# A recommender's product tower on one core: constants, first loads and one copy take other places in the queues

## The reference

```python
for W in (W0, W1):
    last = x.shape[1]
    inter = (x[:, :, None, :] * x_emb[:, None, :, :]).reshape(B, last * F, D)
    x = jnp.einsum('bid,hi->bhd', inter, W)
    outs.append(x.sum(axis=-1))
...
h = jnp.concatenate([z, dense_ctx], axis=1)
h = jnp.maximum(h @ W_top1 + b_top1, 0.0)
h = jnp.maximum(h @ W_top2 + b_top2, 0.0)
y = h @ W_top3
```

## Time and profile before

| | us |
|---|---|
| median of 3 runs | 784.18 |
| lowest and highest run | 783.13, 784.47 |
| the profiled execution | 780.78 |
| its span, first to last instruction | 779.0 |
| TensorE busy in the span | 696.8 |
| VectorE busy | 674.9 |
| GpSimd busy | 501.0 |
| ScalarE busy | 420.2 |

### The profile page before, as it was taken

One profiled execution on the slowest core, in us unless ns is written; L12 is line 12 of the kernel. 1 busy time (PEld: TensorE's weight loads), 2 busy tenths in 40 slices (PEclk: granted clock), 3 DMA queues, 4 the chain that ended last, 5 costly groups with the idle time before them and its releaser, 6 DMA issues.

```text
span 779.0 us, 17028 instructions
## 1 busy us (share of the span) xinstructions
PE 696.8 (89%) x6210; PEld 595.1 (76%) x6210; DVE 674.9 (87%) x864; ACT 420.2 (54%) x769; POOL 501.0 (64%) x406
## 2 busy tenths in 40 slices
PE   0222678999999999999999999999999999999997
PEld 0222455878888888888888888888888888888887
DVE  5653999999999999999999999999999999888810
ACT  0001465656566656557565656655566656575741
POOL 6777887878787877868787887888787850000000
PEclk9999899999999999999999999999999999999999
DMA  4369569696867777787869796777867695854000
GB/s 101 90 156 275 129 184 164 164 171 170 163 167 168 131 185 130 187 134 190 161 163 168 173 162 169 171 148 182 141 171 142 162 160 138 162 153 133 13 7 1
DMA packets 171030, 115.67 MB, mean 148 GB/s; under 512 B 135043, under 2 KB 146906, under 8 KB 170563
## 3 DMA queue, kind: packets, MB, share of 16 engines
q1 hardware_dynamic: 154750, 108.80, 60.3%
q0 software_dynamic: 12800, 3.30, 6.6%
q10 hardware_dynamic: 3397, 2.47, 1.1%
HBM read 104.08 MB, written 15.53 MB: 154 GB/s over the span
## 4 chain that ended last, share of the span: by engine, by line
PE 77%; POOL 7%; DMA 4%; DVE 4%; issue 4%; SPq 3%; ACT 0%; DVEq 0%; ACTq 0%; POOLq 0%
PE z_ps L424 18%; PE x_ps L384 12%; PE x_ps L388 11%; PE x_ps L385 11%; PE g_ps L414 8%; POOL e_rows L360 7%; PE x1T_ps L445 4%; PE aux_ps L373 4%; PE x1T_ps L403 3%; PE x1T_ps L437 2%; SPq L280 2%; PE x1T_ps L435 2%; DVE product_lo L676 2%; DVE products L668 2%; DMA e_scratch<-e_d 2%
## 5 line engine op out<-in xcount | busy, mean ns | idle before, releaser
L360 POOL DMA_INDIRECT e_rows<-in_tbl_dram,ids_sb x400 | 500.6, 1252 | 134.7 <-issue 119.8
L514 ACT CAST product_hi<-products 117x1024 fp32r<-117x1024 f32 (+1 forms) x256 | 242.6, 948 | 102.7 <-DVE products L668 101.7
L676 DVE TENSOR_TENSOR product_lo<-products,product_hi 117x1024 fp32r<-117x1024 f32 (+1 forms) x256 | 277.4, 1084 | 23.1 <-ACT product_hi L514 22.9
L668 DVE TENSOR_TENSOR products<-bases 117x1024 f32<-117x1024 f32 (+1 forms) x256 | 277.5, 1084 | 7.1 <-DMA bases<-eT_scratch 6.5
L384 PE MATMUL x_ps<-product_hi,w_hi 117*128 117x512 f32 x448 | 198.5, 443 | 14.2 <-ACT product_hi L514 10.4
L424 PEld LDWEIGHTS z_ps<-G,w1T 128*128 128x128 f32 x1248 | 165.0, 191 | 17.3 <-issue 0.5
L385 PE MATMUL x_ps<-product_hi,w_lo 117*128 117x512 f32 x448 | 178.2, 398 | 0.0
L424 PE MATMUL z_ps<-G,w1T 128*128 128x128 f32 x1248 | 178.1, 280 | 0.0
L388 PE MATMUL x_ps<-product_lo,w_hi 117*128 117x512 f32 x448 | 148.5, 401 | 19.0 <-DVE product_lo L676 19.0
L388 PEld LDWEIGHTS x_ps<-product_lo,w_hi 117*128 117x128 f32 x448 | 84.3, 190 | 43.6 <-DVE product_lo L676 23.7
L384 PEld LDWEIGHTS x_ps<-product_hi,w_hi 117*128 117x128 f32 x448 | 85.6, 191 | 28.4 <-issue 13.8
(11 more groups left out here) (55 smaller groups left out, 340.1 us busy)
## 6 DMA issues: line engine op xcount, KB each, us to landing
bases<-eT_scratch SPq DMA_DIRECT2D x155, 468.0 KB
e_diag<-e_scratch SPq DMA_DIRECT2D x512, 10.0 KB
id_spread<-id_scratch SPq DMA_DIRECT2D x16, 437.5 KB
e_rows<-in_tbl_dram,ids_sb POOLq DMA_INDIRECT x400
e_scratch<-e_d SPq DMA_DIRECT2D x16, 320.0 KB, 9.5
eT_scratch<-e_rows SPq DMA_DIRECT2D x16, 312.0 KB
eT_scratch<-eT_scratch SPq DMA_DIRECT2D x16, 312.0 KB
w1T<-in_L_rec_W_dram SPq DMA_DIRECT2D x1, 2496.0 KB, 19.3
```

Source lines behind the costliest of these rows:

```text
L360: nc.gpsimd.indirect_dma_start(out=e_rows[t % E_SLOTS][:, f * D:(f + 1) * D], out_offset=None, in_=tables[f], in_offset=bass.IndirectOffse ...
L514: nc.scalar.copy(product_hi[:, first:first + count, :], products[:, first:first + count, :]).then_inc(hi_ready, 1)
L668: nc.vector.tensor_tensor(products[:, first:first + count, :], bases[u % 2][:, b:b + count, cols], bases[u % 2][:, a:a + 1, cols].to_broad ...
L676: nc.vector.tensor_tensor(product_lo[:, first:first + count, :], products[:, first:first + count, :], product_hi[:, first:first + count, : ...
```

## The change

Six transfers of constants (`w1T` and the network's weights and biases) are issued by SP before its wait for the third spread of ids, instead of in chunks 0 and 3 of its loop. The ten first loads of bases for half 0 are all issued by SP, chunk 0's part first; ScalarE issues none and no longer waits for the doubling. The store of e for tile 0 goes behind them, and SP waits until chunk 0's part has landed before it goes into its loop. In the loop, the doubling of the next tile moves behind the diagonal blocks of chunk 1, and the store of e of the next tile from chunk 0 to chunk 2, ahead of the spread of ids. VectorE's copy of e for tile t+1 moves from chunk 0 to chunk 2 of tile t.

```diff
@@ SP, before its loop
                 sp.dma_start(wt1_dense_f[n * GAP:n * GAP + D, :], w_top1[2 * H:2 * H + D, :]).then_inc(wt1_dense_loaded, 16)
+
+            sp.dma_start(w1T[:, :, :], w1).then_inc(w1_loaded, 16)
+            sp.dma_start(wt1_cin[:, :, :], w_top1[0:2 * H, :].rearrange("(k p) n -> p k n", p=128)).then_inc(mlp_loaded, 16)
+            sp.dma_start(wt2[:, :, :], w_top2.rearrange("(k p) n -> p k n", p=128)).then_inc(mlp_loaded, 16)
+            sp.dma_start(wt3[:, :], w_top3).then_inc(mlp_loaded, 16)
+            sp.dma_start(bias1[:, :], b_top1).then_inc(mlp_loaded, 16)
+            sp.dma_start(bias2[:, :], b_top2).then_inc(mlp_loaded, 16)
             spread_ids(2)
             store_eT(0)
-            store_e(0)
             double_eT(0)
             sp.wait_ge(eT_doubled, 16)
-            load_base_part(sp, 0, 0, HB // 2, first_ready[0])
+            for c in range(2):
+                load_base_part(sp, 0, c * (HB // 2), HB // 2, first_ready[c])
+            store_e(0)
+            sp.wait_ge(first_ready[0], 16 * LOADS)
@@ SP, in its loop
                 t, c = divmod(g, CPT)
-                if c == 1 and t + 1 < TILES:
-                    double_eT(t + 1)
                 if g % 2 == 0 and g // 2 + 1 < HALVES:
                     load_bases(g // 2 + 1)
                 spread(g)
-
-                if g == 0:
-                    sp.dma_start(w1T[:, :, :], w1).then_inc(w1_loaded, 16)
-                if g == 3:
...
+                if c == 1 and t + 1 < TILES:
+                    double_eT(t + 1)
                 if c == 0 and t + 1 < TILES:
                     store_eT(t + 1)
+                if c == 2 and t + 1 < TILES:
                     store_e(t + 1)
                 if c == 2 and t + 3 < TILES:
                     spread_ids(t + 3)
@@ ScalarE, before its loop
-            act.wait_ge(eT_doubled, 16)
-            load_base_part(act, 0, HB // 2, HB // 2, first_ready[1])
             round_products(0, 0)
@@ VectorE, in its loop
-                if c == 0 and t + 1 < TILES:
+                if c == 2 and t + 1 < TILES:
                     copy_e(t + 1)
```

## The result

| us | before | changed |
|---|---|---|
| median of the runs shown (4 of each) | 783.65 | 777.75 |
| lowest and highest | 782.56, 784.47 | 777.37, 778.8 |
| the profiled execution | 780.78 | 777.37 |
| its span | 779.0 | 775.6 |

The changed kernel takes 0.9937 of the time before, interval 0.9917 to 0.9956. Two later comparisons gave 0.9949 (0.9926 to 0.9971) and 0.996 (0.9944 to 0.9976), so the gain is 3 to 6 us; the kernel before had medians of 781.5 and 781.7 there, against 783.65 here. The two profiled executions lie 3.4 us apart, since the one before was a quick one of its kind: the traces explain 3.4 us, and the rest is spread between executions.

A forecast was written before the change was run, and what follows sets the result against it. TensorE was taken to bound late tiles, so time could be won only before about 165 us: 17.1 us possible, less 5.6 for gathers and 1.5 for ids, gives 10. Forecast 774 us, 771 to 777 for this case, range 766 to 782.

The forecast's parts named there:

- What bounds: Whole kernel: TensorE sets late tiles, about 42.5 us each; time can be won only before about 165 us.
- Copy of e: VectorE, chunk 0: moving the copy two chunks later removes the 11.12 us wait; its 0.69 us comes back in chunk 2.
- Constants: Six transfers moved to about 19 us, beside gathers: they end at 33 and cost 0, bounds 0 and 6 us.
- First loads by need: Start, half 0: chunk 0's loads land first, VectorE starts at 56.5 instead of 62.49; 6.0 us won, bounds 0 and 6.28.
- From landing to bases: Gathered rows to bases in SBUF: store 5.3, doubling 3.0, five loads 14.3 us; 22.6, or 26 behind other loads.
- Gathers as what is late next: GpSimd, tiles 1 to 3: gathers slow beside busy VectorE, 1.68 us each, and take 5.6 us off the gain.
- The rival in which VectorE shuts the gathers out: About 14 more gathers each wait out a VectorE product, 17 us instead of 4; 784, no change; chance 0.05.
- Store of e: SP, third chunk: about 1 us of issue and 2 of transfer delay ids, costing 1.5 us; bounds 0 and 7.4 per tile.
- The slow rival: SP, last 12 tiles: store of e keeps 6.5 us of issue, ids come late; about 819; chance 0.15.
- Store of e for tile 0 behind the ten loads: SP, start: diagonal loads want this store, but TensorE needs those some 20 us later; costs nothing.
- Late start: Rival: constants end at 46, first products up to 6 us late, tile 3 starts 8 sooner; 777 to 780; chance 0.10.
- The sum: Whole kernel: 17.1 us possible from first loads and copy, less 5.6 for gathers, less 1.5 for ids: 10 won.

The follow-up runs named there:

- e1: Changed kernel with the six constants back in chunks 0 and 3 of SP's loop; 785.1 us, 1.0032 of the kernel before.
- e5: Changed kernel with w1T loaded in chunk 2 and the network's constants in chunk 6 of SP's loop; 791.11 us, 1.0107 of the kernel before.

## Why the prediction was right in side and too large in size

- **What bounds.** Right: the gain is made before 200 us and kept. A late tile is 43.00 of 43 us of TensorE as before, and 577.1 us follow tile 3 in both.
- **Copy of e.** Right: its 11.12 us are gone. VectorE's work from the first products to its request for tile 1 is 108.12 - 2.30 - 67.28 = 38.5, where the prediction had 8.1 + 30.3 = 38.4.
- **Constants: the step that failed.** The prediction took 0, with 6 as the bound, and looked for them in the gathers and the store of rows. It did not count W0, which is loaded on ScalarE's queue in the same stretch: 10.88 us of wait. What they cost in all is the 7.2 us of the first products (67.3 against 60.1) and 4.4 us of the end. SP's six issues for them took 7.6 us (19.02 to 26.66), not under 3, which cost nothing: SP then waited until 35.06.
- **First loads by need.** Right in direction, mis-sized: 6.0 forecast; where the constants do not disturb, 0.9 to 2.4 (60.10 to 61.59 in four kernels, against 62.49). The first part took 11 us from the first issue to VectorE's start (49.05 to 60.10), not 4.5 at the rate of another stage: five more loads are issued right behind it; that they share the engines with it is the likely reason, which no run tested alone.
- **From landing to bases.** 22.9 us forecast for tile 1, 30.6 measured (77.53 to 108.12): the doubling 13.0 instead of 5.3 after the store's issue, doubling 3.3 (3.0), loads 14.3 (14.3). The prediction took the store's time from a place with less in flight, and its three terms add up to 22.6, not 22.9. With the rows stored at 77.53, not 74.6, this is tile 1 at 108.1 instead of 97.5.
- **Gathers as what is late next.** Not from tile 2 on: 28 gathers ran from 80 to 122 us, not 25 (VectorE busy for 37.99 us of them, not 41.77), and tile 2 waited for no bases. For tile 1 their landing was mis-sized. The last one started at 69.62, sooner than the 71.5 forecast, but 3.1 us to landing was too short: without the constants it starts at 70.56 and SP waits for it until 78.18, 7.6 us; with w1T in flight it is 9.6 (71.02 to 80.65 in e1). So most of the 9.85 us does not need w1T in flight. The rival in which VectorE shuts the gathers out does not occur either; the Trainium skill's rule ("SBUF — State Buffer", "Who interferes with whom"), taken to the letter for gathers, is not what this trace shows.
- **Store of e.** Right: 1 us at most in the new place (0.42 median). VectorE's waits for ids are 1.6 to 3.3 us in tile 1 in the three profiles of the changed kernel, where 1.5 was forecast for tiles 2 and 3, and from 180 to 660 us 1.3, 1.6 and 5.4 in all (0.7 before), which cost nothing, as the 577.1 us show. The slow rival, 819, does not occur. The reading that the store was held up by the 64-byte store ahead of it is confirmed by who is held now.
- **Store of e for tile 0 behind the ten loads.** Put at nothing; SP waits 3.0 us for its landing. Without the constants that wait is 3.5 us and SP then still waits 5.6 us for the gathers, so it costs nothing there; whether it does in the changed kernel was not tested.
- **Late start.** This rival, 777 to 780 at a chance of 0.10, came nearest: its time is the one measured, its mechanism (constants in front of tile 0's store) is one half, and W0 the other. That the time agrees is partly luck: it has tile 3 start 8 us sooner, and 3.4 were measured; and it counts from 784.18, where the later comparisons had 781.5 and 781.7 before.
- **The sum.** The 17.1 us possible became 6.2 (11.1 from the copy, less 4.8 at the start and 0.1 of work). Waits took off 2.3 for bases and 1.5 for ids, and 1.0 came back between VectorE's tile 2 and TensorE's tile 3: 3.4. So the miss lies in the start: 6.0 won in the forecast, 4.8 lost as measured; of the 10.8 us between them the constants are 7.2 and the first loads 3.6. The 1.5 us for ids that the forecast takes off at the end are already in tile 3's 182.4; if the same wait is meant, they were taken off twice.

Less than the whole gains nothing that can be told: constants alone 0.999, copy alone 0.9988, constants and first loads without the copy 0.9993, first loads and copy without the constants 1.0032; first loads alone were not run. Together they give 0.994 to 0.996. The traces suggest why: each part takes away the wait into which the others' gain would turn. The three profiles of the changed kernel differ by two waits in tile 1, for bases (2.3, 1.6, 2.8 us) and for ids (1.6, 1.7, 3.3); from VectorE's tile 2 to TensorE's tile 3 all three take 48.3 us. What makes these waits differ was not found.

## What to carry to other kernels

A transfer that moves to a quiet stretch meets everything else that is in flight there, on every queue: list the loads of the other issuing engines and who waits for them before costing it at nothing. Where a chain of transfers (store, doubling, loads) sets the pace, take its durations from a place as busy as the one it will run in. And where several waits are nearly as long as each other, test the parts together as well as alone; here none that was run alone gained.

## What the runs showed that was not expected

- A long stream of small loads is drawn out by large ones beside it: the 34 loads of W0 went out by 32.7 us before and nobody waited for them; beside 3.5 MB of constants on another queue they were awaited until 48.98.
- The transfer issued behind a store in 64-byte pieces is held on its queue until that store is nearly done: 9.20 us for a diagonal load behind it, 0.42 for the store of e that used to stand there and was held 6.5. Small pieces are not the only cause of such a hold: behind w1T, five loads of bases took 9.89 us to issue instead of 4.2 (e5).
- Constants that land some 34 us ahead of a stage (by 44 us, the store at 77.53) can still cost it: the delay went from W0 and the first rows to the loads of bases, and from these to the store of tile 1's rows.
